# V products of two key tiles back to back in an fp32 attention kernel

## The chip, the cores and the metric

One core of a Trainium2 chip. The metric is the device time of one execution in microseconds (us). Everything, the attention of all heads, the feed-forward part and the sums, is one program.

## The reference

Four sequences x of 1024 rows and 128 columns, 16 heads. Cut to what matters:

```
xn = layernorm(x)                                   # (4, 1024, 128)
q, k = rope(xn @ Wq), rope(xn @ Wk); v = xn @ Wv     # q: 16 heads of 64; k and v: 16 heads of 32, each value repeated twice
p = softmax(q @ k^T * scale)                         # (4, 16, 1024, 1024)
attn = (p @ v) @ Wo
ffn = (silu(xn @ Wg^T) * (xn @ Wu^T)) @ Wd^T         # hidden 384, int32 weights / 127
out = x + attn + ffn
```

## The kernel before, in words

After a first part (layer norm, transposes, feed-forward, the projections of the first heads; about 110 us) the attention runs as 32 units. A unit `u` is one sequence, one group of four heads and one half (512) of the queries; four units form one turn of the loop (`pairs_of_steps`, `slot`), the first and the last turn are written out. In a unit the 1024 keys are 8 key tiles `kt` of 128. For each key tile and head TensorE computes transposed scores (128 keys x 512 queries, `score`, line 542) into one of the two PSUM banks `bank_s` (head modulo 2), ScalarE takes exp into `prob` (line 768 for heads 0 and 1 in one instruction of 1024 columns, line 779 for heads 2 and 3, 512 each), and TensorE multiplies by V (`pv`, line 394): eight matmuls in the profile, four heads side by side in strips of 32 columns of the array, accumulating in `bank_o` over all key tiles. `prob` is a ring of 4 key tiles.

The softmax needs each query's maximum ahead: `max_tile` (line 379) computes the scores of the next unit once more, in the other orientation (128 queries x 1024 keys, two matmuls), and VectorE reduces each of 16 such tiles (`reduce_tile`, line 824; two places in PSUM, so tile m waits for the reduction of m - 2). The 16 maxima are split, transposed (`transpose_max`, 386), copied by ScalarE (`read_maxT`, 664) and sent by a DMA into two extra rows of the packed queries (`pack_max`, 246), so that the scores come out with the maximum subtracted.

The softmax's denominators are sums over keys. GpSimd adds the probabilities of the key tiles (`add_probs`, 1011 and 1018): tiles 0 + 1, then 2, 3, the pair 4 + 5 (which VectorE has added: `pair_sum`, 917, in place in `prob`), then 6. Tile 7 is summed by TensorE directly: `denominators` (404 for tile 7, 407 for GpSimd's sum), with ones as weights, again in strips of 32 columns. The result is copied, transposed (`transpose_den`, 414), inverted on VectorE (`invert`, 921), spread and transposed back (`transpose_inv`, 421), and multiplied into the output (`normalise`, 927), which `project_out` (430) multiplies by Wo. All this of unit u - 1 runs inside unit u, the output projection of u - 2 too. `project` (362, three matmuls a chunk) and `project_v` (370, twelve) compute the queries, keys and values of unit u + 4 in the key tiles 6 and 7, in the PSUM banks of the maxima; VectorE rotates them (`rotate`, 815 to 819), ScalarE rounds them (653), GpSimd takes the rest (963).

Nothing is planned at run time: each engine runs a list written out by hand, and waits on semaphores. TensorE's list is `slot`. What orders it against ScalarE is in `score`: heads 2 and 3 wait for the first exp (heads 0, 1) of their key tile, head 0 for the exp of head 2 of the key tile before, and head 1 for that of head 3:

```
EXP_OF = [0, 0, 1, 2]
at_least(pe, prob_ready, NE * (KT * u + kt) + (EXP_OF[h - 2] + 1 if h > 1 else EXP_OF[h + 2] + 1 - NE))
```

In the order before, each key tile issues its scores of heads 0 and 1, then the V product of the key tile before, then heads 2 and 3, with maxima between; by key tile (S0 to S3 scores, M a maximum of two matmuls, PV one V product, P a chunk of projection):

```
0: S0 S1 M PV S2 S3 M M            4: S0 S1 M PV S2 M S3 transpose_den M
1: S0 S1 PV M S2 S3 M project_out M   5: S0 S1 PV M S2 S3 transpose_inv
2: S0 S1 PV M S2 S3 M denominators M  6: S0 S1 P0 PV S2 S3 transpose_max P1
3: S0 S1 M PV S2 M S3 M            7: S0 S1 P2 PV S2 S3 P3 project_v
```

The last turn of the loop has no projections, and the last unit no maxima.

Of the kernel before, what the change touches and what calls it, by code (L numbers as in the profile page):

```python
# [36 lines left out]
HG = 4  # L37
# [3 lines left out]
HALF = S // 2  # L41
# [29 lines left out]

EXP_OF = [0, 0, 1, 2]

INVERT_AFTER = 13


def build(nc, x, tables, w_qkv, wo_even, wo_odd, w_gu, w_down, ident_in, out):
# [10 lines left out]
    with ctx:  # L88
# [24 lines left out]
        y_part = keep("y_part", [128, HALF])  # L113
        o_norm = keep("o_norm", [128, HALF])
        y_acc = keep("y_acc", [128, KT, D])
        wgu = keep("wgu", [128, 2, 2 * HT, 128], F32R)
        wdn = keep("wdn", [128, HT, D])
        qk_pack = [None, None]

        with ExitStack() as early:  # L120
# [15 lines left out]
        with ExitStack() as early:  # L136
            x_all = keep("x_all", [128, NT, D], F32, early)
        prob_sum = keep("prob_sum", [128, 2, HG, HALF])

        xn = [v_sb[min(c // 2, 1)][:, c % 2 * QT:(c % 2 + 1) * QT, :] for c in range(CHUNKS)]  # L140
        wgu_f = y_acc[:, 0:2 * HT, :]
# [49 lines left out]
        def is_first(u):  # L191
            return isinstance(u, int) and u == 0
# [155 lines left out]
        def _(pe):  # L348
# [183 lines left out]
            def slot(i, j, t, last_pair):  # L532
                u, s = 4 * i + 2 * j + t, 2 * i + j
                v, w = u + 1, u + 4
                v_n, v_t = (j, 1) if t == 0 else (1 - j, 0)
                do_max = not (last_pair and j == 1 and t == 1)
                tiles = iter(range(TILES))

                def score(kt, h):

                    at_least(pe, prob_ready, NE * (KT * u + kt) + (EXP_OF[h - 2] + 1 if h > 1 else EXP_OF[h + 2] + 1 - NE))
                    mm(bank_s[:, h % 2, :],  # L542
                       qk_pack[j][0:SCORE_K, 1, kt // QT, h, (kt % QT) * 128:(kt % QT + 1) * 128],
                       qk_pack[j][0:SCORE_K, 0, t, h, :], start=True, stop=True).then_inc(score_ready, 1)

                def pv_before(kt):

                    if kt > 0:
                        pv(u, kt - 1, j)
                    elif not is_first(u):  # L550
                        pv(u - 1, KT - 1, j if t == 1 else 1 - j)

                def maxima():
                    if do_max:
                        m = next(tiles)
                        if m < 2:

                            pe.wait_ge(rope_done, capped(2 * u + 7 + m, 2 * UNITS))
                        max_tile(v, m, v_n, v_t)


                pe.wait_ge(max_packed, 16 * u + 16)
                if isinstance(u, int) and u == 2:

                    pe.wait_ge(filled, 3)
                if do_max and t == 1:

                    pe.wait_ge(packed, 16 * PACKS * (s + 1))
                for kt in range(KT):
                    score(kt, 0)  # L570
                    score(kt, 1)

                    if kt in (0, 3, 4):
                        maxima()
                        pv_before(kt)
                    elif kt < 6:
                        pv_before(kt)
                        maxima()
                    else:
                        if not last_pair:  # L580
                            if kt == 6:

                                pe.wait_ge(max_read, TILES * (v + 1))
                            project(2 * (kt - 6), w, t, s + 2)
                        pv_before(kt)
                    score(kt, 2)
                    if kt in (3, 4):
                        maxima()
                    score(kt, 3)

                    if kt in (0, 1, 2, 3):
                        maxima()
                    if kt == 0:
                        maxima()
                    elif kt == 1:
                        if not is_second(u):
                            project_out(u - 2, 1 - j, s - 1)
                        maxima()
                    elif kt == 2:
                        if not is_first(u):  # L600
                            denominators(u - 1, 1 - t)
                        maxima()
                    elif kt == 4:
                        if not is_first(u):
                            transpose_den(u - 1)
                        maxima()
                    elif kt == 5:
                        if not is_first(u):
                            transpose_inv(u - 1)
                    elif kt == 6:  # L610
                        if do_max:

                            at_least(pe, o_done, u)
                            transpose_max(v)
                        if not last_pair:
                            project(1, w, t, s + 2)
                    elif kt == 7 and not last_pair:
                        project(3, w, t, s + 2)
                        pe.wait_ge(maxT_read, v + 1)
                        project_v(w, t)  # L620

            def body(i, last_pair):
                for j in range(2):
# [1 line left out]
                        slot(i, j, t, last_pair)  # L625

            pairs_of_steps(pe, body)
            pv(UNITS - 1, KT - 1, 1)
            project_out(UNITS - 2, 1, STEPS - 1)
            denominators(UNITS - 1, 1)  # L630
# [6 lines left out]
        def _(act):  # L637
# [109 lines left out]
            def slot(i, j, t, last_pair):  # L747
                u, s = 4 * i + 2 * j + t, 2 * i + j
                first = is_first(u)
                staged = not (last_pair and (j, t) != (0, 0))  # L750
                for kt in range(KT):

                    if not (first and kt < RING):
                        act.wait_ge(pv_done, 8 * u + kt - 3)
                        if kt == 0:
                            act.wait_ge(sum_done, 5 * u - 1)
                        elif kt == 1:
                            act.wait_ge(pair_done, u)
                        elif kt == 2:
                            act.wait_ge(sum_done, 5 * u)  # L760
                        elif kt == 3:
                            act.wait_ge(den_ready, u)
                        elif kt < 6:
                            act.wait_ge(sum_done, 5 * u + 1)
                        else:
                            act.wait_ge(sum_done, 5 * u + kt - 4)
                    act.wait_ge(score_ready, 32 * u + 4 * kt + 2)
                    A(prob[:, kt % RING, 0:2, :], bank_s[:], ACT.Exp).then_inc(prob_ready, 1)  # L768
                    if kt == 0 and not first:
                        read_o(u - 1)  # L770
                    elif kt == 1 and staged:
                        round_hi(0, u + 3, 1 - t, s + 1 + t)
                    elif kt == 2 and not is_second(u):
                        read_y(u - 2)
                    elif kt == 5 and not first:
                        spread_inv(u - 1)
                    for h in (2, 3):
                        act.wait_ge(score_ready, 32 * u + 4 * kt + h + 1)
                        A(prob[:, kt % RING, h, :], bank_s[:, h % 2, :], ACT.Exp).then_inc(prob_ready, 1)  # L779
                    if kt == 0 and not first and staged:  # L780
                        stage_v(u + 3, 1 - t, s + 1 + t)
                    elif kt == 1 and staged:
                        round_hi(1, u + 3, 1 - t, s + 1 + t)
                    elif kt == 2 and not first:
                        read_den(u - 1)
                    elif kt == 6 and not (last_pair and j == 1 and t == 1):
                        read_maxT(u + 1)
# [18 lines left out]
        def _(dve):  # L806
# [106 lines left out]
            def pair_sum(u):  # L913

                dve.wait_ge(prob_ready, NE * (KT * u + 6))
                dve.wait_ge(pv_done, 8 * u + 5)
                V.tensor_tensor(prob[:, 4 % RING], prob[:, 4 % RING], prob[:, 5 % RING], ALU.add).then_inc(pair_done, 1)  # L917

            def invert(u):
                dve.wait_ge(denT_ready, u + 1)  # L920
# [36 lines left out]
        def _(pool):  # L957
# [49 lines left out]
            def add_probs(u, t):  # L1007

                at_least(pool, den_ready, u - 1)
                pool.wait_ge(prob_ready, NE * (KT * u + 2))  # L1010
                TT(prob_sum[:, t], prob[:, 0], prob[:, 1], ALU.add).then_inc(sum_done, 1)  # L1011
                for n, kt in enumerate((2, 3, 4, 6)):
                    if kt == 4:
                        pool.wait_ge(pair_done, u + 1)
                    else:
                        pool.wait_ge(prob_ready, NE * (KT * u + kt + 1))
                    pool.wait_ge(sum_done, 5 * u + n + 1)
                    TT(prob_sum[:, t], prob_sum[:, t], prob[:, kt % RING], ALU.add).then_inc(sum_done, 1)  # L1018

            def add_out(u, t, b):  # L1020

# [80 lines left out]
```

## Time and profile before

| | us |
|---|---|
| runs | 1211.01, 1212.84, 1213.59; median 1212.84 |
| profiled execution | 1210.01, span 1208.2 |
| PE busy | 1161.2 (96%) |
| VectorE, ScalarE, GpSimd busy | 892.1, 697.7, 878.2 |
| mean granted TensorE clock | 0.989 |

The profile is of one execution; its own time is the span of the instructions and 1.8 us around it. In the page's names PE is TensorE's matmuls, PEld its weight loads, DVE VectorE, ACT ScalarE, POOL GpSimd. Matmuls are pipelined: starts of instructions are good, ends are modelled.

### The profile page before, as it was taken

Reading aid. Unit: us, or ns where it says so; the run is one execution under the profiler, and the core shown is the slowest. Engines: PE = TensorE matmul, PEld = TensorE weight load, DVE = VectorE, ACT = ScalarE, POOL = GpSimd, SP = SyncE. Lnnn points to the kernel's source line nnn. Section 1 sums busy time; section 2 is a strip of 40 time slices with the busy share of each in tenths; the row PEclk is TensorE's granted clock in tenths of the full one; section 3 lists DMA queues with packets and bytes.
Section 4 is the critical chain, followed back from the end, with each engine's and each line's share of the span. In section 5 each row is a group of like instructions: output and inputs, shape, how many; then the busy total and the mean of one; then the engine's idle time right before and its main releaser. Section 6 shows DMA issues by size and latency. Waiting matters only on the chain.

```text
span 1208.2 us, 19402 instructions
## 1 busy us (share of the span) xinstructions
PE 1161.2 (96%) x6288; PEld 642.0 (53%) x6288; DVE 892.1 (74%) x1009; ACT 697.7 (58%) x1074; POOL 878.2 (73%) x274
## 2 busy tenths in 40 slices
PE   5898999999999999999999999999999999999985
PEld 4786455555555555555555555555555555554432
DVE  7685778777777778777777777777777777876622
ACT  3333556666666656666666656666666556665563
POOL 2312777887778877787777887787777887787775
PEclk9898999999999999999999999999999999999997
DMA  6652707062421517062422517061422517050000
GB/s 222 172 238 99 213 2 217 1 188 65 142 76 62 156 36 215 0 197 55 141 75 74 143 36 215 0 202 49 148 68 87 131 36 215 0 125 1 4 1 17
DMA packets 56287, 124.58 MB, mean 103 GB/s; under 512 B 7968, under 2 KB 19488, under 8 KB 54048
## 3 DMA queue, kind: packets, MB, share of 16 engines
q1 hardware_dynamic: 56224, 123.89, 35.0%
q8 instruction: 21, 0.34, 0.1%
q14 instruction: 42, 0.34, 0.1%
HBM read 53.08 MB, written 10.49 MB: 53 GB/s over the span
## 4 chain that ended last, share of the span: by engine, by line
PE 90%; DVE 3%; POOL 2%; ACT 1%; issue 1%; DMA 1%; SPq 1%; POOLq 0%; ACTq 0%; DVEq 0%
PE bank_s L542 24%; PE scores L379 22%; PE bank_o L394 20%; PE scores L362 7%; PE bank_m L370 3%; PE bank_m L404 3%; PE bank_m L430 2%; PE bank_m L407 2%; POOL prob_sum L1018 2%; PE scores L480 2%; PE bank_s L497 1%; PE bank_m L414 1%; PE bank_m L421 1%; DVE prob L917 1%; DMA x_all<-x 1%
## 5 line engine op out<-in xcount | busy, mean ns | idle before, releaser
L824 DVE TENSOR_REDUCE row_max<-scores 128x1 f32<-128x1024 f32 x512 | 605.7, 1217 | 194.7 <-PE scores L379 194.7
L1018 POOL TENSOR_TENSOR prob_sum<-prob_sum,prob 128x2048 f32<-128x2048 f32 x128 | 586.3, 4581 | 112.9 <-DVE prob L917 103.8
L542 PE MATMUL bank_s<-qk_pack 98*128 98x512 f32 x1024 | 383.6, 432 | 12.8 <-ACT prob L768 6.7
L779 ACT ACTIVATE prob<-bank_s 128x512 f32<-128x512 f32 x512 | 285.1, 596 | 172.3 <-PE bank_s L542 165.1
L768 ACT ACTIVATE prob<-bank_s 128x1024 f32<-128x1024 f32 x256 | 262.5, 1025 | 187.8 <-PE bank_s L542 180.5
L379 PE MATMUL scores<-qk_pack 96*128 96x512 f32 x1024 | 340.5, 419 | 1.1 <-DVE row_max L824 1.1
L542 PEld LDWEIGHTS bank_s<-qk_pack 98*128 98x128 f32 x1024 | 183.0, 189 | 232.4 <-ACT prob L768 144.3
L394 PE MATMUL bank_o<-prob,v 128*32 128x512 f32 x2048 | 273.6, 606 | 0.9 <-ACT prob L779 0.9
L379 PEld LDWEIGHTS scores<-qk_pack 96*128 96x128 f32 x1024 | 177.0, 190 | 136.8 <-DVE row_max L824 109.1
L963 POOL TENSOR_TENSOR qk_stage<-rope,qk_stage 128x512 fp32r<-128x512 f32 x64 | 82.1, 1283 | 90.8 <-ACT qk_stage L653 90.8
L1011 POOL TENSOR_TENSOR prob_sum<-prob 128x2048 f32<-128x2048 f32 x32 | 146.4, 4575 | 0.0
L362 PE MATMUL scores<-x_stage,w_stage 128*128 128x512 f32 x336 | 100.0, 406 | 0.0
L394 PEld LDWEIGHTS bank_o<-prob,v 128*32 128x32 f32 x2048 | 40.3, 108 | 89.4 <-issue 88.0
L1026 POOL TENSOR_TENSOR y_acc<-y_part,y_acc 128x512 f32<-128x512 f32 x32 | 41.1, 1285 | 56.9 <-ACT y_part L745 56.9
L917 DVE TENSOR_TENSOR prob<-prob 128x2048 f32<-128x2048 f32 x32 | 75.7, 2364 | 0.0
L817 DVE TENSOR_TENSOR rope<-scores,table 128x512 f32<-128x512 f32 x64 | 43.9, 686 | 42.2 <-PE scores L362 42.1
L362 PEld LDWEIGHTS scores<-x_stage,w_stage 128*128 128x128 f32 x336 | 59.4, 189 | 15.2
L734 ACT COPY den<-bank_m 128x512 f32<-128x512 f32 x32 | 18.8, 586 | 52.0 <-PE bank_m L407 52.0
L815 DVE TENSOR_TENSOR scores<-scores,table 128x512 f32<-128x512 f32 x64 | 44.3, 692 | 3.1 <-PE scores L362 2.5
L819 DVE TENSOR_TENSOR rope<-scores,rope 128x512 f32<-128x512 f32 x64 | 44.3, 692 | 2.2
L370 PEld LDWEIGHTS bank_m<-w_stage,x_stage 128*128 128x128 f32 x336 | 41.8, 191 | 2.4
L653 ACT CAST qk_stage<-rope 128x512 fp32r<-128x512 f32 x64 | 39.2, 616 | 4.1 <-DVE rope L819 4.1
(88 smaller groups left out, 679.5 us busy)
## 6 DMA issues: line engine op xcount, KB each, us to landing
qk_pack<-qk_stage SPq DMA_DIRECT2D x384, 128.0 KB, 3.5
table<-tables SPq DMA_DIRECT2D x16, 2048.0 KB, 9.9
w_stage<-w_scratch SPq DMA_DIRECT2D x14, 640.0 KB, 4.7
v<-v_stage SPq DMA_DIRECT2D x32, 256.0 KB, 3.2
xT_scratch<-xT_hl SPq DMA_DIRECT2D x4, 1024.0 KB, 9.5
x_stage<-xT_scratch SPq DMA_DIRECT2D x4, 1024.0 KB, 5.4
w_scratch<-w_split SPq DMA_DIRECT2D x1, 2560.0 KB, 15.1
x_all<-x SPq DMA_DIRECT2D x4, 512.0 KB, 12.5
```

What stands on the lines that cost most here:

```text
L362: last = mm(scores[:, c, :], w_from[:, a, c, :], x_from[:, r, cols], start=n == 0, stop=n == 2)
L370: last = mm(bank_m[:, j * 128:(j + 1) * 128], x_from[:, r, at:at + 128], w_from[:, a, 4, :], start=n == 0, stop=n == 2)
L379: last = mm(scores[:, 2 * (m % places) + c, :], qk_pack[n][0:SPLIT_K, 0, t, h, (m % QT) * 128:(m % QT + 1) * 128], qk_pack[n][0:SPLIT_K, 1 ...
L394: last = mm(bank_o[h * E:(h + 1) * E, :], v_sb[n][:, kt, h * E:(h + 1) * E], prob[:, kt % RING, h, :], start=kt == 0, stop=kt == KT - 1)
L542: mm(bank_s[:, h % 2, :], qk_pack[j][0:SCORE_K, 1, kt // QT, h, (kt % QT) * 128:(kt % QT + 1) * 128], qk_pack[j][0:SCORE_K, 0, t, h, :], s ...
L768: A(prob[:, kt % RING, 0:2, :], bank_s[:], ACT.Exp).then_inc(prob_ready, 1)
L779: A(prob[:, kt % RING, h, :], bank_s[:, h % 2, :], ACT.Exp).then_inc(prob_ready, 1)
L824: V.tensor_reduce(row_max[:, m:m + 1], scores[:, at:at + 2, :].rearrange("p c k -> p (c k)"), axis=AX.X, op=ALU.max).then_inc(max_read, 1)
L917: V.tensor_tensor(prob[:, 4 % RING], prob[:, 4 % RING], prob[:, 5 % RING], ALU.add).then_inc(pair_done, 1)
L963: TT(qk_stage[:, 2 * k + 1, t, :], rope[:, 2 * k, :], qk_stage[:, 2 * k, t, :].bitcast(F32), ALU.subtract).then_inc(lo_done, 1)
L1011: TT(prob_sum[:, t], prob[:, 0], prob[:, 1], ALU.add).then_inc(sum_done, 1)
L1018: TT(prob_sum[:, t], prob_sum[:, t], prob[:, kt % RING], ALU.add).then_inc(sum_done, 1)
```

## The change

Four things change. TensorE's list: the V products of two key tiles are issued together, in key tiles 0, 2, 4 and 6 (key tile 0 issues tiles 6 and 7 of the unit before), and the denominators stand right behind the pair of key tile 2. The maxima are placed anew, and the projection's chunks too; chunk 0 waits for 15 reductions instead of 16. The pair sum writes a buffer of its own, `prob_pair`, for which two weight buffers of the first part move into memory shared with it. ScalarE's small copies change places, and VectorE inverts after maximum 9 instead of 13. The new order:

```
0: S0 S1 M PV PV S2 M S3 M                      4: S0 S1 M M PV PV S2 S3 M
1: S0 S1 project_out M S2 M S3                  5: S0 S1 M M transpose_inv S2 S3 M
2: S0 S1 M M PV PV denominators S2 S3 M         6: S0 S1 P0 PV PV S2 transpose_max P1 S3
3: S0 S1 M M transpose_den S2 S3                7: S0 S1 P2 S2 P3 S3 project_v
```

```diff
-INVERT_AFTER = 13
+INVERT_AFTER = 9
...
+        prob_pair = keep("prob_pair", [128, HG, HALF])
...
-                def pv_before(kt):
+                def pv_pair(kt):
                     if kt > 0:
+                        pv(u, kt - 2, j)
                         pv(u, kt - 1, j)
                     elif not is_first(u):
+                        pv(u - 1, KT - 2, j if t == 1 else 1 - j)
                         pv(u - 1, KT - 1, j if t == 1 else 1 - j)
...
+                def project_chunk(c):
+                    if not last_pair:
+                        pe.wait_ge(max_read, TILES * v + TILES - 1 + c // 2)
+                        project(c, w, t, s + 2)
...
                 for kt in range(KT):
                     score(kt, 0)
                     score(kt, 1)
+                    if kt == 0:
                         maxima()
+                        pv_pair(kt)
+                        score(kt, 2)
                         maxima()
+                        score(kt, 3)
                         maxima()
+                    elif kt in (2, 4):
+                        maxima(2)
+                        pv_pair(kt)
+                        if kt == 2 and not is_first(u):
+                            denominators(u - 1, 1 - t)
+                        score(kt, 2)
+                        score(kt, 3)
+                        maxima()
                     elif kt == 1:
                         if not is_second(u):
                             project_out(u - 2, 1 - j, s - 1)
                         maxima()
+                        score(kt, 2)
                         maxima()
+                        score(kt, 3)
+                    elif kt == 3:
+                        maxima(2)
                         if not is_first(u):
                             transpose_den(u - 1)
+                        score(kt, 2)
+                        score(kt, 3)
...
                     elif kt == 6:
+                        project_chunk(0)
+                        pv_pair(kt)
+                        score(kt, 2)
                         if do_max:
                             at_least(pe, o_done, u)
                             transpose_max(v)
+                        project_chunk(1)
+                        score(kt, 3)
+                    else:
+                        project_chunk(2)
+                        score(kt, 2)
+                        project_chunk(3)
+                        score(kt, 3)
                         if not last_pair:
+                            pe.wait_ge(maxT_read, v + 1)
+                            project_v(w, t)
...
# exps (ScalarE)
-                        if kt == 0:
-                            act.wait_ge(sum_done, 5 * u - 1)
-                        elif kt == 1:
+                        if kt < 2:
                             act.wait_ge(pair_done, u)
...
-                    if kt == 0 and not first:
-                        read_o(u - 1)
+                    if kt == 0 and not first and staged:
+                        stage_v(u + 3, 1 - t, s + 1 + t)
...
-                    elif kt == 5 and not first:
+                    elif kt == 4 and not first:
                         spread_inv(u - 1)
...
-                    if kt == 0 and not first and staged:
-                        stage_v(u + 3, 1 - t, s + 1 + t)
+                    if kt == 0 and not first:
+                        read_o(u - 1)
...
# pair_sum (VectorE)
-                dve.wait_ge(pv_done, 8 * u + 5)
-                V.tensor_tensor(prob[:, 4 % RING], prob[:, 4 % RING], prob[:, 5 % RING], ALU.add).then_inc(pair_done, 1)
+                at_least(dve, sum_done, 5 * u - 1)
+                V.tensor_tensor(prob_pair[:], prob[:, 4 % RING], prob[:, 5 % RING], ALU.add).then_inc(pair_done, 1)
...
# add_probs (GpSimd)
-                    TT(prob_sum[:, t], prob_sum[:, t], prob[:, kt % RING], ALU.add).then_inc(sum_done, 1)
+                    part = prob_pair[:] if kt == 4 else prob[:, kt % RING]
+                    TT(prob_sum[:, t], prob_sum[:, t], part, ALU.add).then_inc(sum_done, 1)
```

## Rows read from the trace of the kernel before

**Rows 1.** The page, part 1 (busy us, share, instructions); part 5, V's loads.
```profile
PE 1161.2 (96%) x6288; PEld 642.0 (53%) x6288; DVE 892.1 (74%) x1009; ACT 697.7 (58%) x1074; POOL 878.2 (73%) x274
...
L394 PEld LDWEIGHTS bank_o<-prob,v 128*32 128x32 f32 x2048 | 40.3, 108 | 89.4 <-issue 88.0
```

**Rows 2.** Busy time by stretch; columns are in the first row.
```profile
core 0: us, PE busy (x) PEld busy (x) DVE busy (x) ACT busy (x) POOL busy (x), PEclk, DMA share, GB/s
621.00:655.00 34.00, 33.98 (x186) 18.28 (x186) 26.51 (x28) 20.79 (x32) 26.82 (x9) 1.00 0.00 1
100.00:140.00 40.00, 35.86 (x173) 21.51 (x171) 25.20 (x27) 19.88 (x29) 22.30 (x8) 0.91 0.67 206
```

**Rows 3.** Chain of waits, 587 to 656 us: start, us, what.
```profile
587.09 0.53 PE bank_s L542 x2
...
589.73 0.92 PE scores L379 x4
...
593.87 0.89 PE bank_m L430 x8
594.76 0.47 PE scores L379 x2
595.70 0.99 PE bank_o L394 x8
596.70 0.67 PE scores L379 x2
598.31 0.99 PE bank_m L404 x8
599.30 0.86 PE bank_m L407 x8
...
619.01 0.70 PE scores L362 x3
619.71 1.29 PE bank_m L370 x12
621.00 0.53 PE bank_s L542 x2
```

**Rows 4.** List of waits, 600 to 1140 us: us in total, times, longest.
```profile
PEld bank_s L542 <- ACT prob L768: 69.6, 80, 1.4
...
PEld bank_s L542 <- ACT prob L779: 27.0, 84, 0.8
```

**Rows 5.** Timeline of PE, 600 to 614 us: start, us, what.
```profile
601.11 0.63 PE L379 MATMUL scores<-qk_pack 96*128 96x512 f32 x2
601.67 1.06 PE L394 MATMUL bank_o<-prob,v 128*32 128x512 f32 x8
602.67 0.50 PE L542 MATMUL bank_s<-qk_pack 98*128 98x512 f32 x1
...
610.70 0.63 PE L542 MATMUL bank_s<-qk_pack 98*128 98x512 f32 x2
611.17 0.60 PE L421 MATMUL bank_m<-ident,den 128*128 128x128 f32 x4
611.79 0.99 PE L542 MATMUL bank_s<-qk_pack 98*128 98x512 f32 x2
612.61 0.91 PE L362 MATMUL scores<-x_stage,w_stage 128*128 128x512 f32 x3
```

**Rows 6.** Timeline of the weight loads, same place.
```profile
611.78 0.19 PEld L542 LDWEIGHTS bank_s<-qk_pack 98*128 98x128 f32 x1 [0.25 <-ACT prob L779]
612.27 0.19 PEld L542 LDWEIGHTS bank_s<-qk_pack 98*128 98x128 f32 x1 [0.30 <-ACT prob L779]
```

**Rows 7.** Timeline of ACT, same place.
```profile
611.13 1.09 ACT L779 ACTIVATE prob<-bank_s 128x512 f32<-128x512 f32 x2 [0.37 <-PE bank_s L542]
612.81 1.02 ACT L768 ACTIVATE prob<-bank_s 128x1024 f32<-128x1024 f32 x1 [0.59 <-PE bank_s L542]
```

**Rows 8.** Timeline, 613 to 621 us: pair sum, addition behind it.
```profile
613.42 2.28 DVE L917 TENSOR_TENSOR prob<-prob 128x2048 f32<-128x2048 f32 x1
...
615.87 9.27 POOL L1018 TENSOR_TENSOR prob_sum<-prob_sum,prob 128x2048 f32<-128x2048 f32 x2 [3.23 <-DVE prob L917]
...
620.84 0.69 PE L542 MATMUL bank_s<-qk_pack 98*128 98x512 f32 x2
```

**Rows 9.** Timeline in the last unit, 1178 to 1184 us.
```profile
1178.86 4.56 POOL L1018 TENSOR_TENSOR prob_sum<-prob_sum,prob 128x2048 f32<-128x2048 f32 x1
...
1180.74 4.84 DVE L917 TENSOR_TENSOR prob<-prob 128x2048 f32<-128x2048 f32 x1
...
1182.30 0.30 PEld L542 LDWEIGHTS bank_s<-qk_pack 98*128 98x128 f32 x2 [1.11 <-ACT prob L768]
...
1183.97 0.19 PEld L542 LDWEIGHTS bank_s<-qk_pack 98*128 98x128 f32 x1 [0.30 <-ACT prob L779]
```

**Rows 10.** Weight loads where the unit 31 begins.
```profile
1125.64 0.19 PEld L542 LDWEIGHTS bank_s<-qk_pack 98*128 98x128 f32 x1 [0.95 <-DMA qk_pack<-max_rows]
```

More of the change, by code:

```diff
@@ L115, in build @@
         y_acc = keep("y_acc", [128, KT, D])
-        wgu = keep("wgu", [128, 2, 2 * HT, 128], F32R)
-        wdn = keep("wdn", [128, HT, D])
         qk_pack = [None, None]
@@ L138, in build @@
         prob_sum = keep("prob_sum", [128, 2, HG, HALF])
+        with ExitStack() as early:
+            wgu = keep("wgu", [128, 2, 2 * HT, 128], F32R, early)
+            wdn = keep("wdn", [128, HT, D], F32, early)
+        prob_pair = keep("prob_pair", [128, HG, HALF])
         xn = [v_sb[min(c // 2, 1)][:, c % 2 * QT:(c % 2 + 1) * QT, :] for c in range(CHUNKS)]
@@ L544, in score, with maxima @@
                        qk_pack[j][0:SCORE_K, 0, t, h, :], start=True, stop=True).then_inc(score_ready, 1)
-                def pv_before(kt):
+                def pv_pair(kt):
                     if kt > 0:
+                        pv(u, kt - 2, j)
                         pv(u, kt - 1, j)
                     elif not is_first(u):
+                        pv(u - 1, KT - 2, j if t == 1 else 1 - j)
                         pv(u - 1, KT - 1, j if t == 1 else 1 - j)
-                def maxima():
-                    if do_max:
+                def maxima(n=1):
+                    for _ in range(n if do_max else 0):
                         m = next(tiles)
@@ L571, in slot @@
                     score(kt, 1)
-                    if kt in (0, 3, 4):
+                    if kt == 0:
                         maxima()
-                        pv_before(kt)
-                    elif kt < 6:
-                        pv_before(kt)
+                        pv_pair(kt)
+                        score(kt, 2)
                         maxima()
[L579 to L587, printed above, removed]
-                        maxima()
-                    score(kt, 3)
-                    if kt in (0, 1, 2, 3):
-                        maxima()
-                    if kt == 0:
+                        score(kt, 3)
+                        maxima()
+                    elif kt in (2, 4):
[5 more added lines that the diff above has]
+                        score(kt, 3)
                         maxima()
@@ L598, in slot @@
                         maxima()
-                    elif kt == 2:
-                        if not is_first(u):
-                            denominators(u - 1, 1 - t)
+                        score(kt, 2)
                         maxima()
-                    elif kt == 4:
+                        score(kt, 3)
+                    elif kt == 3:
+                        maxima(2)
                         if not is_first(u):
                             transpose_den(u - 1)
-                        maxima()
+                        score(kt, 2)
+                        score(kt, 3)
                     elif kt == 5:
+                        maxima(2)
                         if not is_first(u):
                             transpose_inv(u - 1)
+                        score(kt, 2)
+                        score(kt, 3)
+                        maxima()
                     elif kt == 6:
+                        project_chunk(0)
+                        pv_pair(kt)
+                        score(kt, 2)
                         if do_max:
@@ L614, in slot @@
                             transpose_max(v)
-                        if not last_pair:
[L616 to L620, printed above, removed]
+                        project_chunk(1)
+                        score(kt, 3)
+                    else:
+                        project_chunk(2)
+                        score(kt, 2)
+                        project_chunk(3)
+                        score(kt, 3)
+                        if not last_pair:
+                            pe.wait_ge(maxT_read, v + 1)
+                            project_v(w, t)
             def body(i, last_pair):
@@ L627, in _ @@
             pairs_of_steps(pe, body)
+            pv(UNITS - 1, KT - 2, 1)
             pv(UNITS - 1, KT - 1, 1)
@@ L754, in slot @@
                         act.wait_ge(pv_done, 8 * u + kt - 3)
-                        if kt == 0:
-                            act.wait_ge(sum_done, 5 * u - 1)
-                        elif kt == 1:
+                        if kt < 2:
                             act.wait_ge(pair_done, u)
```

## The prediction

> **What bounds the kernel now.** I read the page's busy line first [rows 1]: PE 96%, DVE 74%, POOL 73%, ACT 58%. Matmul ends are modelled, so 96% may hide waits; the stage table of one unit in the middle says the same with the clock at 1.00 [rows 2]. The chain of waits over such a unit [rows 3] runs from one matmul group to the next, and its first and last rows, both the pair of scores that opens a unit, are 621.00 - 587.09 = 33.91 us apart. There are 32 units; 27 of them (2 to 28) have this length. The order of work on PE therefore sets the time, and with it two things: how often PE changes between full matmuls (128 columns of weights) and blocks with 32 columns (V products, denominators), and how often a score matmul has to wait for an exp, which the list of waits counts 80 and 84 times between 600 and 1140 us [rows 4].
>
> **What a joined block saves.** Below, a head is the stretch from a key tile's second score matmul to its third, a tail the stretch from the third to the next key tile's second. In the chain the eight matmuls of a V product take 0.99, and the two full matmuls behind take 0.67, where two take 0.47 elsewhere: 1.19 for a product alone. Where two blocks stand back to back, the denominators' parts, the second costs 0.86 [rows 3]. Joining saves 1.19 - 0.86 = 0.33. Before, there are nine blocks in a unit (eight products, the denominators). After, there are four: pairs in key tiles 0, 2, 4, 6, the denominators directly behind the one in 2. Five joins at 0.33 are 1.65 us a unit, some 53 us over 32 units. Bounds: nothing, or all 1.19 each (6.0 a unit); the row of the adjacent blocks is the same pattern, so I take 0.33.
>
> One doubt is whether the second product's weight loads still hide: the denominators' weights are all ones, the products' differ. A full matmul brings its own load of 0.19, and a run of four of them takes 0.92, 0.23 each [rows 3, 6]: loads hide behind matmuls in flight here, whatever they hold. If the four loads of 0.11 [rows 1] of a joined product did not, a join would save 0.33 - 0.44 = -0.11. The Trainium skill speaks for that ("TensorE: Matmul & The Clock Gate", Part 3, The mechanism): a load overlaps running matmuls only where its row group is another one, and V products use all rows. By that rule the time would be that of the last rival below; the trace speaks against it.
>
> **What the maxima covered.** The scores of heads 2, 3 go into the same two banks as those of heads 0, 1, so the third score matmul waits for the first exp of its key tile (two heads at once), and the next key tile's first and second wait for the second and third exp. Their least lengths are in the trace:
> - Tail: third score matmul 610.70, exp 611.13 (0.43 later), the next tile's two loads at 611.78 and 612.27, both waiting for ACT [rows 5 to 7]: 1.57. Behind a block the first full matmul takes 0.1 longer: 1182.30 to 1183.97, 1.67 [rows 9]. From the fourth score matmul it is 0.43 + exp 0.60 + 0.05 = 1.08.
> - Head: 612.27 to the exp at 612.81 is 0.54, the exp 1.02, 0.05 to the load: 1.61 (1.50 where the second matmul hadn't waited).
> - Fill: 0.23 a full matmul; 0.34 for the one behind a block or behind a wait (611.79 + 0.49 is 612.28, next group at 612.61); from the last full matmul before a block to the first after it 1.32 (601.34 to 602.67) [rows 5], a pair 1.32 + 0.86 = 2.18, pair and denominators 2.18 + 4 x 0.43 = 3.90; four transposes about 0.36 (they start 0.11 apart); a projection chunk 0.70, V's projection 1.29, the output projection 0.89 [rows 3].
>
> The new order, each the larger of fill and least length, in us:
> - Heads of key tiles 0 to 7: 2.65 (a maximum, pair); 1.70 (output projection, maximum, behind a wait); 5.09 (two maxima, the second waiting shortly for DVE, pair, denominators); 1.76 (two maxima, transposes); 3.22; 1.77; 2.99 (projection chunk, pair); 1.63 (one chunk fills only 1.04, so the least length holds). Sum 20.8.
> - Tails: 1.89 (fourth score 0.81 behind the third, + 1.08); 1.78 (0.70 + 1.08); 1.68; 1.58; 1.68; 1.58; 2.23 (transposed maxima, chunk 1 and the fourth score: 1.15 + 1.08); 2.87 (chunk 3, V's projection). Sum 15.3.
>
> That is 36.1 us a unit. Tails 2 to 5 hold at most two scores, one maximum (two matmuls) and two scores, 1.2 to 1.3 of fill against 1.58 to 1.68, and tail 3 has no maximum at all, 0.8 against 1.58. Tail 6 issues chunk 1 before the fourth score, so that its exp starts late and 0.6 is lost behind it; head 7 has lost its V product and loses another 0.6. The score waits add up to 3.5 us, and each stalled matmul's successor costs another 0.11. The same addition over the order of before gives 33.7 against 33.9 measured: there each head holds a V product (1.32 and more) and most tails two maxima.
>
> **The other edits.** The pair sum's own buffer takes away its wait for the fifth V product, and lets exps of the next unit start on the pair sum, not on POOL's addition behind it. In the 27 middle units neither was late: the addition begins at 615.87 and takes 4.6, ending near 620.5, just before the next unit's first score matmul at 620.84 [rows 8]; gain there 0, from -0.1 to 0.2. DVE has more to do at once (two maxima issued together), its last maximum ends at about 27.8 of the unit and the pair sum at about 31.3, 2.7 later than now; POOL's two additions behind end 4.4 into the next unit, where the denominators want them at 12: hidden. Reciprocal after maximum 9 and copies moved on ACT: ACT has 20.8 busy of 34 [rows 2] and they stand beside PE; 0, or 0.6 each if one landed ahead of an exp that is late. Chunk 0's wait is relaxed by one maximum: it is still 0.1 to 0.2 after its reduction. The moved weight buffers cost nothing: they belong to the start.
>
> **Sum.** Units 2 to 28: 27 x (36.1 - 33.9) = +59; if my addition is short by the same 0.15 as before, +64; I take 62. Unit 1: +2. Units 29 to 31 have no projections; their end is the maxima's transpose, copy and DMA (first score load of the next unit waits for it, 0.95 us idle [rows 10]); that transpose comes behind key tile 6's third score, 29.7 against 27.5 now: +2.1 each, +6. The last unit's end hangs on pair sum and POOL. Now the pair sum takes 4.84 there instead of 2.28, because it began at 1180.74 under an addition of POOL that ran from 1178.86 to 1183.42 [rows 9]; it took 2.28 where POOL was idle [rows 8]. After, it begins later with less of that left: +0.5, from 0 to 2.6. Together +71, on the profiled execution's 1210.0 (1208.2 span and 1.8 around it): 1281. The median shown is 2.8 above that execution: 1284.
>
> **Rivals.**
> - The joins pay and the waits stay hidden (faster): 1212.8 - 53 = 1160. For it: 96% busy, and a join is a sure 0.33. Decides where the exps of a tail take under 1.25, the fill of two scores, a maximum and two scores. Against it: 1.57 and 1.67 in rows 5 to 8. 5%.
> - Half of the stalls: the load behind a waiting one is ready (no 0.11), and ACT's three exps come closer together than 0.49. Per unit +1.1 instead of +2.2: 1212.8 + 35 = 1248. Nothing in the trace shows it. 7%.
> - The clock: where PE was often idle, from 100 to 140 us, the granted clock was 0.91 [rows 2]. If the new gaps (0.6 at most, ten a unit) did that in all units, 30 us of PE work a unit would take up to 3.0 longer: up to 1284 + 32 x 3 = 1380. Against it: the gaps there were 2 us, and stalls of 0.3 to 0.5 in the middle leave it at 1.00. 4%.
> - Loads of a joined product exposed: five joins that cost 0.11 instead of saving 0.33 are 2.2 a unit, 70 over 32: 1354. Against it rows 3. 1%.
> - No effect (within 0.2%, about what a measurement of this kernel can tell): gain and loss would have to meet at 1.65. 2%.
>
> **How the numbers follow.** The forecast has 81%; its own range is 1262 to 1302 (a stall more or less of 0.5 a unit is 16 us). The range of 80% goes down towards the second rival: 1256 to 1303. Faster 5%, same 2%, slower 93%.
>
> **What would show it.** V products in groups of 16 matmuls with 1.85 to 1.9 in the chain (right: the join), units of about 36 us; the waits of scores for exps up from 97 us in 600:1140 to some 150 or more; in the chain more ACT; key tile 3 to 4 with two loads waiting in a row and 1.57 between third and second score. I am wrong if units are under 33.9, if tails 2 to 5 take about 1.25, or if the clock in the middle isn't 1.00.

## The result and the profile after

The changed kernel takes 1287.22 us (median of 4, 1286.35 to 1287.75) against 1212.42 before: ratio 1.0617, interval 1.0598 to 1.0635. It is 75 us slower; forecast were 1284 and slower. Its profiled execution took 1286.35, span 1284.5.

The page's busy line and two stage tables of the kernel after [rows 1, 2]: one middle unit, and where unit 30 ends and 31 begins. Columns of the tables are start:end and length, busy us of PE, PEld, DVE, ACT, POOL with counts, granted clock, DMA share, GB/s.

```profile
PE 1194.6 (93%) x6288; PEld 647.6 (50%) x6288; DVE 885.2 (69%) x1009; ACT 699.6 (54%) x1074; POOL 876.5 (68%) x274
```
```profile
729.00:765.00 36.00, 34.49 (x185) 18.14 (x185) 26.24 (x27) 20.87 (x32) 26.50 (x9) 1.00 0.10 30
...
1190.00:1204.00 14.00, 12.12 (x51) 5.00 (x44) 5.83 (x7) 6.48 (x12) 9.06 (x2) 0.76 0.02 6
```

The instructions are the same in number, and the other engines' busy times moved by under 1%; PE's busy time grew by 33 us with no work added, because a busy matmul contains waits (22 of the 33 lie in units 2 to 28, at full clock; the rest is where the clock was lower for stretches, see the end of the step-by-step part). The share fell to 93%: in a window of 36 us in the middle 1.5 us are now visibly idle, at full clock.

The chain of waits over one unit after (start, us, what), which answers to [rows 3]:

```profile
728.70 0.52 PE bank_s L544 x2
729.22 0.47 PE scores L381 x2
729.69 1.85 PE bank_o L396 x16
...
738.39 1.85 PE bank_o L396 x16
740.25 0.86 PE bank_m L406 x8
741.10 0.86 PE bank_m L409 x8
741.96 0.66 PE bank_s L544 x2
742.63 0.47 PE scores L381 x2
743.10 0.97 PE bank_s L544 x2
744.07 1.07 PE scores L381 x4
745.14 0.44 PE bank_m L416 x4
745.58 0.26 PE bank_s L544
745.84 0.02 issue
745.86 0.60 ACT prob L792
746.46 0.04 issue
746.51 0.98 PE bank_s L544 x2
...
759.92 0.60 ACT prob L792
760.52 0.04 issue
760.57 0.51 PE bank_s L544
761.08 0.02 issue
761.11 1.03 ACT prob L781
762.14 0.04 issue
762.18 0.50 PE bank_s L544
...
764.90 0.51 PE bank_s L544 x2
```

Read it so: a pair of products is one row of 1.85 = 0.99 + 0.86, the two parts of the denominators 0.86 each, and full matmuls behind 0.66. From the opening scores to the next unit's it is 764.90 - 728.70 = 36.20 us. Exps now stand in the chain, which had none in the middle of a unit: at 736.22 (left out above), behind the fourth score of key tile 1, where no maximum follows; at 745.86, between key tiles 3 and 4, where no maximum is left in the tail; at 759.92, behind the late fourth score of key tile 6; and at 761.11 in head 7, which lost its product. The page's chain gives ACT 8% where it was 1%. Two scores that took 0.47 take 0.97 or 0.98 where both wait (743.10, 746.51).

The weight loads of that place, answering to [rows 6]:

```profile
745.31 0.30 PEld L544 LDWEIGHTS bank_s<-qk_pack 98*128 98x128 f32 x2
746.50 0.19 PEld L544 LDWEIGHTS bank_s<-qk_pack 98*128 98x128 f32 x1 [0.89 <-ACT prob L792]
746.99 0.19 PEld L544 LDWEIGHTS bank_s<-qk_pack 98*128 98x128 f32 x1 [0.30 <-ACT prob L792]
```

Third score 745.34, the next tile's second 746.99: 1.65, where 1.58 was forecast as the least a tail can take.

The list of waits between 600 and 1140 us, which answers to [rows 4]:

```profile
PEld bank_s L544 <- ACT prob L792: 81.9, 178, 0.9
...
PEld bank_s L544 <- ACT prob L781: 18.2, 33, 0.9
```

Together 100.1 us, against 96.6 before: the rise to 150 or more, which the prediction named as a sign, did not come. The list counts idle time of weight loads, also where matmuls in flight hide it, as behind each V product before. What moved is its composition: waits for the exps of heads 2 and 3 went from 27.0 us (84 times) to 81.9 (178 times), those for the first exp from 69.6 to 18.2.

By unit, from the first score matmul of each: unit 1 39.14 (before 36.12); units 2 to 28 36.20 (33.89); units 29 to 31 33.70, 35.47, 36.27 (31.69, 32.39, 32.44); the last with all behind it 52.4 (50.1).

### The profile page after: what moved, and what is told of

Read it like the earlier page. It is cut to its first block, busy times and chain, and to the rows that moved or that the text cites. A ratio compares the mean times of both kernels' runs of the same rounds, so it can differ in the third digit from the quotient of the medians.

```text
span 1284.5 us, 19473 instructions
## 1 busy us (share of the span) xinstructions
PE 1194.6 (93%) x6288; PEld 647.6 (50%) x6288; DVE 885.2 (69%) x1009; ACT 699.6 (54%) x1074; POOL 876.5 (68%) x274
## 3 DMA queue, kind: packets, MB, share of 16 engines
q1 hardware_dynamic: 56224, 123.89, 33.1%
## 4 chain that ended last, share of the span: by engine, by line
PE 86%; ACT 8%; issue 2%; DVE 1%; DMA 1%; POOL 1%; SPq 1%; POOLq 0%; ACTq 0%; DVEq 0%
PE bank_s L544 27%; PE scores L381 20%; PE bank_o L396 19%; PE scores L364 5%; ACT prob L792 5%; ACT prob L781 3%; PE bank_m L372 3%; PE bank_m L406 2%; PE bank_m L409 2%; PE bank_m L432 2%; PE scores L482 1%; PE bank_s L499 1%; PE bank_m L423 1%; PE bank_m L416 1%; DMA x_all<-x 1%
## 5 line engine op out<-in xcount | busy, mean ns | idle before, releaser
L544 PE MATMUL bank_s<-qk_pack 98*128 98x512 f32 x1024 | 440.8, 465 | 60.8 <-ACT prob L792 38.6
L792 ACT ACTIVATE prob<-bank_s 128x512 f32<-128x512 f32 x512 | 290.8, 596 | 366.0 <-PE bank_s L544 357.4
L1032 POOL TENSOR_TENSOR prob_sum<-prob_sum,prob 128x2048 f32<-128x2048 f32 x96 | 439.1, 4573 | 10.1 <-ACT prob L792 1.3
L381 PE MATMUL scores<-qk_pack 96*128 96x512 f32 x1024 | 321.0, 412 | 0.0
L1032 POOL TENSOR_TENSOR prob_sum<-prob_sum,prob_pair 128x2048 f32<-128x2048 f32 x32 | 146.3, 4572 | 175.3 <-DVE prob_pair L930 175.3
L396 PE MATMUL bank_o<-prob,v 128*32 128x512 f32 x2048 | 253.8, 614 | 0.0
L381 PEld LDWEIGHTS scores<-qk_pack 96*128 96x128 f32 x1024 | 183.7, 191 | 58.9 <-DVE row_max L837 34.4
L396 PEld LDWEIGHTS bank_o<-prob,v 128*32 128x32 f32 x2048 | 54.3, 111 | 128.2 <-issue 100.2
L364 PE MATMUL scores<-x_stage,w_stage 128*128 128x512 f32 x336 | 100.1, 406 | 0.0
L930 DVE TENSOR_TENSOR prob_pair<-prob 128x2048 f32<-128x2048 f32 x32 | 73.1, 2284 | 1.7 <-ACT prob L792 1.7
```

Of the source, the lines that this page charges most:

```text
L364: last = mm(scores[:, c, :], w_from[:, a, c, :], x_from[:, r, cols], start=n == 0, stop=n == 2)
L381: last = mm(scores[:, 2 * (m % places) + c, :], qk_pack[n][0:SPLIT_K, 0, t, h, (m % QT) * 128:(m % QT + 1) * 128], qk_pack[n][0:SPLIT_K, 1 ...
L396: last = mm(bank_o[h * E:(h + 1) * E, :], v_sb[n][:, kt, h * E:(h + 1) * E], prob[:, kt % RING, h, :], start=kt == 0, stop=kt == KT - 1)
L544: mm(bank_s[:, h % 2, :], qk_pack[j][0:SCORE_K, 1, kt // QT, h, (kt % QT) * 128:(kt % QT + 1) * 128], qk_pack[j][0:SCORE_K, 0, t, h, :], s ...
L930: V.tensor_tensor(prob_pair[:], prob[:, 4 % RING], prob[:, 5 % RING], ALU.add).then_inc(pair_done, 1)
L1032: TT(prob_sum[:, t], prob_sum[:, t], part, ALU.add).then_inc(sum_done, 1)
```

## The experiments

Each was run against the kernel before on the same chip. "Kernel after" is the changed one. An order is written by key tile as ahead of the prediction, with short names: PO is `project_out`, D the denominators, TD, TI and TM are `transpose_den`, `transpose_inv` and `transpose_max`, P a chunk, V `project_v`. Lengths of heads and tails of runs are medians over units 3 to 28.

**1. Products taken apart.**

```diff
 # key tiles 0 to 7 of the kernel after
-0: S0 S1 M PV PV S2 M S3 M          +0: S0 S1 M PV S2 M S3 M
-1: S0 S1 PO M S2 M S3               +1: S0 S1 PV PO M S2 M S3
-2: S0 S1 M M PV PV D S2 S3 M        +2: S0 S1 M M PV D S2 S3 M
-3: S0 S1 M M TD S2 S3               +3: S0 S1 M M PV TD S2 S3
-7: S0 S1 P2 S2 P3 S3 V              +7: S0 S1 P2 PV S2 P3 S3 V       (4, 5, 6 alike)
```

> The changed kernel with its V products taken apart again: one product in each key tile's head, as before the change, the denominators behind the one in key tile 2; maxima, chunks and everything else stay where the change put them. Theory (the tails' waits for exps cost the time, joins save 0.33 each): four joins are lost, 1.3 us a unit, but the heads of key tiles 1, 3, 5 and 7 become longer and those of 0, 2, 4, 6 shorter, and head 7's wait of 0.6 is covered: units of 36.5 us against 36.2, about 1299 us. Rival 1 (placing two products in one head costs the time): units fall towards 33.9, about 1215. Rival 2 (the second product's loads are exposed, a join costs 0.11): units of 34.8, about 1240.

Measured: 1301.99 us (ratio to before 1.0750, 1.0734 to 1.0766), units of 36.89. Joins do save time: taking them apart costs 0.7 a unit. By head it shows directly: a head that lost the second product of its pair became 0.82 to 0.86 shorter, and heads 1, 3 and 5, where the product now stands alone, 1.13 to 1.33 longer; head 7, which had been waiting, only 0.51. Both rivals fell. The unit came out 0.4 longer than I had added up (units 9, 13, 17, 21 and 25, at 37.5 to 37.8, longer still), and the chain shows where: small matmuls directly behind a 32-column block.

```profile
707.41 1.06 PE bank_o L409 x8
708.47 1.09 PE bank_m L445 x8
...
719.08 0.99 PE bank_o L409 x8
720.08 0.59 PE bank_m L429 x4
```

The eight matmuls of the output projection take 1.09 there against 0.89 [rows 3], four transposes 0.59 against 0.44 in the kernel after.

Units 30 and 31 take 34.4 here, where the kernel after takes 35.5 and 36.3, and the granted clock is 1.00 from 1110 to 1290 us; this bears on run 9.

**2. The chunks' places.**

```diff
-6: S0 S1 P0 PV PV S2 TM P1 S3
-7: S0 S1 P2 S2 P3 S3 V
+6: S0 S1 P0 PV PV S2 S3 TM P1
+7: S0 S1 P2 P3 S2 S3 V
```

> The changed kernel with projection chunk 1 behind the fourth score of key tile 6 instead of ahead of it, and chunk 3 in the head of key tile 7 instead of in its tail. Theory: the late fourth score of tail 6 and the empty head 7 cost 0.6 each; both are mended, units of 34.9 to 35.0 instead of 36.2, about 1250 us. Rival (the chunks' place doesn't matter, what costs is the key tiles 2 to 5 alone, or DVE's later chain): 1287, or less than half of that gain.

Measured: 1255.6 us (ratio 1.0366, 1.0346 to 1.0387), units of 34.99. Two instruction groups moved by a few places give back 32 of the 75 us. The chain of that kernel in key tiles 6 and 7: no exp is left in it.

```profile
736.69 1.85 PE bank_o L409 x16
738.54 0.67 PE bank_s L557 x2
739.21 0.11 PE bank_m L401
739.32 0.70 PE scores L377 x3
740.02 0.63 PE bank_s L557 x2
740.65 1.38 PE scores L377 x6
742.03 0.47 PE bank_s L557 x2
742.50 1.29 PE bank_m L385 x12
```

**3 and 4. Shorter exps**, in the kernel before and in the kernel after. The second half of the columns of heads 2 and 3 keeps the constant 1 from unit 1 on; these two kernels leave that half of the exps out.

```diff
+                    cut = HALF // 2
...
-                        A(prob[:, kt % RING, h, :], bank_s[:, h % 2, :], ACT.Exp)
+                        A(prob[:, kt % RING, h, 0:cut], bank_s[:, h % 2, 0:cut], ACT.Exp)
```

> The kernel before with the exps of heads 2 and 3 taken over 256 of 512 columns (half of their work is left out, so 0.38 us each instead of 0.60; unit 1 does a little more). Theory: the order of before waits little for exps, and what its waits are then comes from DVE: units of 33.2 instead of 33.9, about 1196 us. Rival (ScalarE is not what scores wait for): 1212.

> The changed kernel with the same shorter exps of heads 2 and 3. Theory: every tail of key tiles 1 to 6 ends with these exps, so the changed kernel gains about three times what the one before does: units of 34.7 instead of 36.2, about 1242 us; what stays is the wait in head 7, which is the first exp's. Rival (joins are expensive or DVE sets the end): it gains no more than the kernel before, 1270.

Measured, one run each: 1196.9 and 1244.3 us; units 33.2 to 33.3 and 34.9. Before gains 14 us and after 43, from the same cut and with TensorE's list untouched. That is three times as much in all, but the middle units show a factor of two: 33.88 to 33.28, and 36.20 to 34.93. The rest of the ratio comes from the end, where the kernel before became slower by it (unit 31 33.9 instead of 32.4, the last 54.1 instead of 50.1; the cause is open). The exps of heads 2 and 3 are what the tails wait for: tails of key tiles 2 to 5, 1.65 to 1.68 long, went to about 1.30. In 2, 4 and 5 the fill is then the bound; tail 3, which has no maximum, still waits 0.24 for the exp. In the kernel before, tail 5, which was at 1.57, went to 1.21. Head 7 stayed at 1.62, since it waits for the first exp. Heads 2, 3, 5 grew by 0.2 to 0.4, now waiting for VectorE's reductions: the next bound behind the exps.

**5. The own buffer and its waits alone**, on the kernel before.

```diff
-                        if kt == 0:
-                            act.wait_ge(sum_done, 5 * u - 1)
-                        elif kt == 1:
+                        if kt < 2:
                             act.wait_ge(pair_done, u)
...
-                V.tensor_tensor(prob[:, 4 % RING], prob[:, 4 % RING], prob[:, 5 % RING], ALU.add)
+                V.tensor_tensor(prob_pair[:], prob[:, 4 % RING], prob[:, 5 % RING], ALU.add)
```

> The kernel before with the pair sum's own buffer and the waits that go with it, alone: TensorE's list, ScalarE's copies and VectorE's inversion stay as before. Theory: in the 27 middle units nothing waited for the pair sum's place, so units stay at 33.9; in the last turn, where the exp of key tile 0 waited up to 1.5 us for GpSimd's addition, some 0 to 3 us are gained: 1208 to 1211 where the kernel before has 1210.5. Rival (the buffer or its waits cost in the changed kernel): slower than before by more than 5 us.

Measured: 1208.7 us (ratio 0.9975, 0.9966 to 0.9984; 11 runs). Units 2 to 28 are at 33.87, units 30 and 31 at 31.91 instead of 32.4. The medians differ by 2.8 us; the two profiled executions differ by 1.2, of which 1.0 lies in units 30 and 31, and where the rest of the 2.8 lies is not shown. It is no part of the loss.

**6 to 8. The same work, placed by the least lengths.** All three have the own buffer and the changed kernel's places of `read_o` and `stage_v` on ScalarE; order of 6, 7, 8:

```
6 (single)                          7 (pairs)                        8 (mixed)
0: S0 S1 M PV S2 S3 M M             0: S0 S1 M PV PV S2 M S3 M       0: S0 S1 M PV PV S2 S3 M M
1: S0 S1 PV M S2 S3 PO M            1: S0 S1 M PO S2 S3 M M          1: S0 S1 PV S2 S3 M M
2: S0 S1 M PV S2 M S3 M D           2: S0 S1 PV PV S2 M S3 D         2: S0 S1 PO M S2 S3 M D
3: S0 S1 M PV S2 S3 M M             3: S0 S1 M M TD S2 S3 M          3: S0 S1 M M PV M S2 S3 TD M
4: S0 S1 PV M S2 S3 TD M            4: S0 S1 M PV PV S2 M S3 M       4: S0 S1 M PV S2 S3 M M
5: S0 S1 M PV S2 S3 M M             5: S0 S1 M TI S2 S3 M M          5: S0 S1 PV M S2 S3 M TI
6: S0 S1 PV TI P0 S2 S3 P1 TM P2    6: S0 S1 PV PV S2 S3 P0 P1 TM    6: S0 S1 PV PV S2 S3 TM P0 P1
7: S0 S1 PV P3 S2 S3 V              7: S0 S1 P2 P3 S2 S3 V           7: S0 S1 P2 P3 S2 S3 V
```

```diff
-INVERT_AFTER = 9
+INVERT_AFTER = 12      # 6; 8 in 7; 9 in 8
...
-                    elif kt == 4 and not first:
+                    elif kt == 5 and not first:       # 6 and 8; 7: behind the exps of key tile 3
                         spread_inv(u - 1)
```

> One product in each key tile as before, the denominators alone, own buffer, but maxima, transposes and chunks placed so that every head and every tail holds at least its least length (two maxima in the tails of key tiles 0, 3, 5, one maximum and a block or a transpose in the others, chunks 0 and 3 in heads, 1 and 2 in the tail of 6). By the addition of fill and least lengths: 32.6 a unit against 33.7 by the same addition for before, so -1.1 x 31 = -35 us: 1176. Rival (the order of before is already at what PE's work allows, its waits have another cause): 1210.

> All products in pairs in the heads of key tiles 0, 2, 4, 6, as in the changed kernel, denominators alone in the tail of key tile 2, maxima and chunks placed so that tails and odd heads are filled as far as there is work for it. By the addition: 33.0 a unit, -0.75 x 31 = -23 us against before: 1187. If joins are what makes the changed kernel slow, this one stays above 1250.

> Pairs only in the heads of key tiles 0 and 6, single products in 1, 3, 4, 5, none in 2 and 7, where the output projection with a maximum, and chunks 2 and 3, fill the head; tails with two maxima, or a maximum and denominators or a transpose. By the addition: 32.1 a unit, -1.6 x 31 = -50 us against before: 1160. If joins save nothing it is that of the single order, 1176 or more; if the least lengths were wrong, about 1210 or above.

Measured: 1179.0 us (0.9730, 0.9715 to 0.9744), 1195.5 (0.9869, 0.9845 to 0.9892), 1182.4 (0.9759, 0.9743 to 0.9775). Their usual middle units are 32.79, 33.0 and 32.32, against additions of 32.6, 33.0 and 32.1. So all products in pairs, the pattern of the changed kernel, are faster than before once tails and odd heads are filled. They are still 16 us slower than single products placed with the same care: most of the gain over the kernel before comes from the placing, not from joins. Joining only where a head has other fill takes 0.5 a unit off the single order; the two also differ in the places of maxima and transposes, so the 0.5 is not the joins' alone. Order 7 missed its 1187 by 8 us, and the mixed order as a whole its 1160 by 22, for two reasons that the addition didn't hold. Units 5, 6, 13, 14, 21 and 22 of the mixed order take 34.0 to 35.0 (some 11 us over the others), and in its last turn units 30 and 31 take 33.6 and 34.3 and the last 52.5, where unit 29 takes 31.5. The usual units' 0.2 over the addition are another 5 us. TensorE's timeline where unit 21 ends:

```profile
800.82 0.74 PE L557 MATMUL bank_s<-qk_pack 98*128 98x512 f32 x2 [1.64 <-DMA qk_pack<-max_rows]
801.39 0.63 PE L394 MATMUL scores<-qk_pack 96*128 96x512 f32 x2
801.95 3.49 PE L409 MATMUL bank_o<-prob,v 128*32 128x512 f32 x16
```
```profile
794.00:802.00 8.00, 6.36 (x38) 4.98 (x39) 5.09 (x7) 3.59 (x7) 6.45 (x2) 1.00 0.63 161
802.00:806.00 4.00, 4.00 (x19) 1.12 (x19) 1.22 (x1) 1.10 (x3) 2.67 (x1) 0.57 0.00 0
```

In the shorter unit the DMA of the maxima's rows, issued at 798.21 behind the packing of keys and V on SP's queue, comes 1.64 late; and right behind that idle time the granted clock is 0.57 (mostly its lower level, 1.2 GHz), and the pair takes 3.49 instead of 1.9. This is read from the trace: no run moved that DMA. Order 7 has the same wait where unit 6 begins (1.23 us at 279.03).

**9 and 10. The last turn**: the kernel after, and order 8, with two products in the head of key tile 0, none in that of 5 and one in each other for units 29 to 32.

```diff
+LAST = ["S0 S1 M PV PV S2 S3 M M", "S0 S1 PV M S2 S3 PO M", "S0 S1 M PV S2 S3 M D M", "S0 S1 M PV S2 S3 M TD M",
+        "S0 S1 M PV S2 S3 M M", "S0 S1 M S2 S3 TI M", "S0 S1 PV S2 S3 TM", "S0 S1 PV S2 S3"]
-                    for op in ORDER[kt].split():
+                    for op in (LAST if last_pair else ORDER)[kt].split():
```

> The changed kernel, but in the last turn of the loop (units 29 to 32, without projections) one product stands in the head of each key tile except 5, as before the change. Theory: the changed order leaves head 7 of those units empty, PE idles over 1 us three times within a few us, the granted clock falls to about half, and pair and denominators run slow: that is why units 30 and 31 took 35.5 and 36.3 us instead of the 34.5 that the terms gave. With products in heads 6 and 7 these units take 31.5 to 32.5 and the clock stays above 0.95 there: 8 to 10 us less, 1278. Rival (the clock falls for another reason, or the long first heads are waits): less than 4 us.

> The mixed order (pairs in key tiles 0 and 6) with the same last turn of single products. Middle units stay at 32.3 with two of eight at 34.0, where the DMA of the maxima's rows comes 1.6 late and the clock falls behind it; units 29 to 31 take 31.5 to 32 instead of 31.4, 33.6, 34.3: 3 to 5 us less than the 1182 of the mixed order, 1178. Rival as for the changed kernel: no gain.

Measured: 1274.0 us (ratio 1.0511, 1.0492 to 1.0530) and 1171.8 (0.9693, 0.9648 to 0.9737). Units 29 to 31 take 31.7, 31.9, 31.9 in both. The first gains 13 us where 8 to 10 were forecast: 9.8 in units 29 to 31, and 4.1 in the last unit, which the forecast left out. The second gains 11 where 3 to 5 were forecast: 3.7 in units 29 to 31, 4.5 in the last unit, and the rest in the middle, where units 5 and 6 took 33.1 and 32.4. Where the kernel after has 0.76, run 9 has (same columns):

```profile
1190.00:1204.00 14.00, 13.19 (x76) 6.54 (x70) 7.68 (x7) 8.60 (x13) 9.66 (x3) 1.00 0.02 6
```

The second is the fastest kernel of this study, 3.1% under the one before. Its last turn is not the best one here: units 29 to 31 of order 6 take 30.6 to 30.8. The two were not put together.

## Why the prediction was right, step by step

- *Order on PE sets the time, units of 33.9.* Right: units 2 to 28 went from 33.89 to 36.20, 27 x 2.31 = 62 us; 62 were forecast.
- *A join saves 0.33.* Right in size: a pair is one row of 1.85, as 0.99 + 0.86. The doubt about exposed weight loads is settled by the same row, since the second product, with other weights than the first, costs as little as the denominators did. The saving shows by itself only in run 1: 1.13 to 1.33 for a product alone, 0.82 to 0.86 for one joined.
- *Tails are held at 1.58 and 1.68.* Right: measured 1.65 to 1.68 in key tiles 2 to 5. Where transposes stand ahead of the third score, 1.65 and not 1.58: its exp starts 0.09 later (0.52 behind the score, not 0.43). Runs 3 and 4 show the cause: with shorter exps the same tails take 1.3.
- *Tail 6 and head 7 lose 0.6 each.* Right: 2.23 and 1.61 measured, 2.23 and 1.63 forecast, and run 2 took both back.
- *Sum of heads and tails 20.8 + 15.3.* Measured 20.8 + 15.4.
- *The other edits cost nothing in the middle.* Right; run 5 puts the buffer and its waits at -3 us. The pair sum ran from 757.34 to 759.62 in that unit and ended 31.1 behind the unit's first score (31.3 were forecast). GpSimd waited up to 5.5 us for it; neither TensorE nor ScalarE did. The moved copies and the inversion were not run by themselves (in the order of before the inversion after maximum 9 would wait for a transpose that stands behind maxima which wait for it); since heads and tails came out within 0.2 a unit of the addition, which gives them nothing, little is left for them.
- *Unit 1 +2, units 29 to 31 +2.1 each, the end +0.5.* Here the sizes were off: +3.0; +2.0, +3.1, +3.8; +2.3. Together 14 instead of 9. The profiled execution took 1286.35 where 1281 had been added up, 5 more, which is just this. That the median, 1287, came within 3 of the forecast 1284 is in part luck: the 2.8 added for a median above its profiled execution was 0.9 here. Units 29 to 31 held the term that I had named as a rival and put at 4%: the clock. Not in the middle, but where head 7 stands empty and the maxima's DMA is awaited. The kernel after, its timeline as unit 31 begins:

```profile
1194.38 1.16 PE L544 MATMUL bank_s<-qk_pack 98*128 98x512 f32 x2 [1.20 <-ACT prob L781]
1195.89 1.19 PE L544 MATMUL bank_s<-qk_pack 98*128 98x512 f32 x2 [0.35 <-ACT prob L792]
1196.88 1.05 PE L381 MATMUL scores<-qk_pack 96*128 96x512 f32 x2
1197.87 3.60 PE L396 MATMUL bank_o<-prob,v 128*32 128x512 f32 x16
1201.40 0.50 PE L544 MATMUL bank_s<-qk_pack 98*128 98x512 f32 x1
```

  The pair takes 3.60, twice its 1.92, between an idle 1.20 and 0.35 ahead of it and a group at full speed behind; in run 9 the longest idle time at this place is 0.54 and the pair takes 1.92. The heads of key tile 0 of units 30 and 31 took 3.92 and 4.94 where unit 29's took 2.64, and the three units' excess of 2.6 over the forecast is about this. For unit 1 I have no experiment of its own. In the last unit the pair sum took 2.29 and not 4.84, since POOL had just finished, so the forecast collision went away. The clock was low there too (0.57 from 1232 to 1236, 0.63 from 1249 to 1263, where the kernel before has 1.00 from 1158 to 1180 of its last unit), and run 9 took 4.1 off this unit although its pair sum took 4.83 again; how much of the +2.3 each part makes stays open.
- *Signs.* Pairs of 1.85, units of 36.2, more ACT in the chain, and two loads waiting in a row between key tiles 3 and 4 all came. The waits of scores for exps did not rise to 150 us but stayed at 100.1: as a sum over loads they are no measure of what a reordering costs, since they also hold waits that matmuls hide.
- *Rivals.* The faster one (1160) fell in runs 3 and 4: what decides is the exps' 1.6, not their fill. "Half of the stalls" (1248) fell: the load behind a waiting one came 0.49 later (746.50 and 746.99), and tails 2 to 5 all took 1.65 to 1.68. The exposed loads (1354) fell with the 1.85.

## What to carry to other kernels

Where two PSUM banks are shared by four score tiles, each stretch between a score and the one that reuses its bank has a least length (score, exp, hand-over; here 1.6 us), and other work on the bounding engine costs nothing until it has filled the stretch. List the stretches and write fill against least length, and a reordering can be priced before it is built: here five of six came within 1%, and the mixed order missed by 2%. A saving by joining blocks (0.33 each here) is real, but taking a block out of a stretch that it filled costs more than the join gives; join only where other work can take its place. Once the units are shorter, look at the queue that nobody waited for before, and at the clock behind every new idle time of more than a microsecond.

## What was unexpected of the hardware

- Small matmuls (128 columns) directly behind a 32-column block run slower: eight in 1.09 instead of 0.89, four transposes in 0.59 instead of 0.44.
- The granted clock fell behind idle times of PE of 1.2 us and more, mostly at the ends of units: in the kernel after (0.76 over 14 us), in run 8 (0.57 over 4 us), in run 7 (0.79 over 8 us from 1105), in runs 2 and 10 too. It did not fall behind the shorter waits of up to 0.6 that come many times a unit in the kernel after, nor in the last units of the kernel before up to 1180 us. Nor does every such idle time bring it down. In run 4:

```profile
1158.78 0.73 PE L544 MATMUL bank_s<-qk_pack 98*128 98x512 f32 x2 [1.20 <-ACT prob L781]
```
```profile
1157.00:1165.00 8.00, 6.47 (x34) 3.32 (x34) 3.35 (x4) 4.19 (x9) 6.84 (x2) 1.00 0.04 11
```

  In run 3 the clock stayed at 1.00 behind 1.77 us of idle time at 1077, too. What decides between the two was not measured.
- A pair sum on DVE that begins under an addition of POOL takes about as long as the rest of that addition more (4.84 instead of 2.28 [rows 9]). The other runs have the same at other overlaps: 3.49 with 1.34 of the addition left in run 1, 3.83 with 1.69 in run 7, 5.65 with 3.50 in run 3. In the kernel after, begun when POOL was idle, it took 2.29 in the same unit.
